# A gated delta-rule decoder layer: outputs and gate kept transposed, factors applied at the eviction, a new order on every queue

## The reference

```python
q, k, v = split(silu(conv4(x @ w_qkv)));  z = x @ w_z          # 16 q/k heads, 32 v heads, 128 channels each
for t in tokens:                                               # per batch and v head
    S = S * exp(g_t);  delta = (v_t - k_t S) * b_t
    S = S + outer(k_t, delta);  o_t = q_t S
og = o * silu(z)
on = og * rsqrt(mean(og * og, -1) + 1e-6) * norm_w
attention = on.reshape(B, T, 32 * 128) @ w_out                 # sum over heads
```

## Time and profile before

| | us |
|---|---|
| median of three runs (lowest, highest) | 2197.31 (2196.64, 2201.70) |
| the profiled execution, own time | 2197.97 |
| its span | 2196.2 |
| attention part, steady: first L1520 of m = 0 to that of m = 53 | 199.0 to 1428.9 |
| drain, to the first L1520 of m = 63 | 1428.9 to 1651.6 |
| cross attention and experts | 1651.6 to 2196.2 |

### The profile page before, as it was taken

One profiled execution on the slowest core, in us unless ns is written; L12 is line 12 of the kernel. 1 busy time (PEld: TensorE's weight loads), 2 busy tenths in 40 slices (PEclk: granted clock), 3 DMA queues, 4 the chain that ended last, 5 costly groups with the idle time before them and its releaser, 6 DMA issues.

```text
span 2196.2 us, 49295 instructions
## 1 busy us (share of the span) xinstructions
PE 2018.6 (92%) x18636; PEld 1681.6 (77%) x18636; DVE 1723.7 (78%) x2944; ACT 1497.9 (68%) x3523; POOL 893.3 (41%) x714
## 2 busy tenths in 40 slices
PE   4648999999999999999999999998878899999998
PEld 3437888888888888888888888887765567666676
DVE  6789798898988889898898988975236777767665
ACT  4536877778777787777878778765667666665632
POOL 1623454454454544544544545432343213322232
PEclk8869999999999999999999999998989999999999
DMA  3422323323233323323233232211342022222232
GB/s 79 96 70 50 81 57 69 83 55 67 63 74 71 68 65 67 74 65 75 64 61 79 63 70 71 42 49 48 87 148 87 1 97 73 82 96 97 83 129 87
DMA packets 274633, 161.56 MB, mean 74 GB/s; under 512 B 209352, under 2 KB 246752, under 8 KB 269280
## 3 DMA queue, kind: packets, MB, share of 16 engines
q1 hardware_dynamic: 274400, 158.41, 27.6%
HBM read 122.43 MB, written 35.91 MB: 72 GB/s over the span
## 4 chain that ended last, share of the span: by engine, by line
issue 35%; POOL 27%; PE 22%; DVE 9%; ACT 4%; DMA 2%; SPq 1%; POOLq 0%; DVEq 0%; ACTq 0%
POOL Q L557 5%; POOL SM L579 5%; POOL EB L495 5%; PE ps L1735 4%; POOL SZ L581 4%; PE ps L1351 3%; POOL EB L499 3%; PE ps L1352 2%; PE ps L1353 2%; POOL WL L473 2%; POOL SM L587 2%; ACT SC L860 2%; PE ps L1647 1%; PE ps L1656 1%; PE ps L1484 1%
## 5 line engine op out<-in xcount | busy, mean ns | idle before, releaser
L913 DVE SCALAR_TENSOR_TENSOR A<-ps,CW,A 128x508 f32<-128x508 f32 (+2 forms) x768 | 517.1, 735 | 62.7 <-ACT A L676 59.9
L574 POOL TENSOR_SCALAR SM<-SM 128x8 f32<-128x8 f32 x64 | 12.7, 198 | 746.8 <-ACT DL L695 746.8
L1351 PE MATMUL ps<-XH,WH 128*128 128x512 f32 x512 | 223.2, 436 | 31.9 <-DVE A L913 31.0
L1484 PE MATMUL ps<-WO,DL 128*128 128x256 f32 x1008 | 232.7, 384 | 19.0 <-ACT DL L682 11.6
L1484 PEld LDWEIGHTS ps<-WO,DL 128*128 128x128 f32 x1008 | 193.3, 193 | 47.9 <-ACT DL L682 13.4
L1353 PE MATMUL ps<-XH,WL 128*128 128x512 f32 x512 | 208.1, 407 | 0.0
L1352 PE MATMUL ps<-XL,WH 128*128 128x512 f32 x512 | 207.5, 405 | 0.0
L695 ACT ACTIVATE DL<-SZ 128x128 f32<-128x128 f32 x512 | 152.9, 300 | 59.4 <-issue 32.6
L1131 DVE TENSOR_TENSOR SZ<-SZ,ps 128x512 f32<-128x512 f32 x128 | 86.6, 687 | 128.4 <-PE ps L1520 126.9
L860 ACT ACTIVATE SC<-ps,A 128x128 f32<-128x128 f32 x512 | 142.2, 387 | 51.3 <-DVE A L1256 50.7
L1116 DVE TENSOR_TENSOR BP<-ps,EB 128x512 f32<-128x512 f32 x256 | 158.4, 682 | 2.6 <-ACT EB L667 2.6
(11 more groups left out here) (223 smaller groups left out, 5530.7 us busy)
## 6 DMA issues: line engine op xcount, KB each, us to landing
EB<-decay_rows SPq DMA_DIRECT2D x128, 256.0 KB, 4.6
WE<-expert_halves SPq DMA_DIRECT2D x32, 1024.0 KB, 5.1
x_blocks<-BP SPq DMA_DIRECT2D x256, 32.0 KB, 1.7
X<-x_blocks SPq DMA_DIRECT2D x16, 512.0 KB, 5.8
tt_blocks<-TI SPq DMA_DIRECT2D x16, 512.0 KB, 2.6
tn_blocks<-TM SPq DMA_DIRECT2D x16, 512.0 KB, 2.6
TTF<-tt_blocks SPq DMA_DIRECT2D x256, 32.0 KB, 1.9
expert_halves<-BP SPq DMA_DIRECT2D x8, 1024.0 KB, 5.5
```

What stands on the lines that cost most here:

```text
L913: dve.scalar_tensor_tensor(acc, ps(i, 0, [[128, 4], [1, 128 - s]]), at(CW, tile * 4 + 3 - s, [[1, 1]]), acc, ALU.mult, ALU.add).then_inc(s ...
L1351: pe.matmul(out, sa, ma, start=(kt == 0), stop=False)
L1484: t = pe.matmul(ps(7 - i, b * 256, [[1, 256]]), at(on_buf(k), (4 * i + 2 * b + v) * 128, [[1, 128]]), at(WO, v * 256, [[1, 256]]), start=( ...
```

## The change

z is computed transposed (weights stationary, 512 tokens moving; one bank for each head), the outputs too (deltas stationary), so that the gated output needs no transposing before the output projection. The factor 1/rms is not applied to it; PE projects each head by itself (no accumulation over the two heads; head 0 in banks 4 and 5, head 1 in 6 and 7), and the factor comes in at the eviction: ACT writes head 0 scaled to DL, POOL adds that to Y, DVE multiplies head 1 and adds it. The sums of squares over channels, which now lie on partitions, are made on PE with PICK, copied by ACT, transposed by PE, and scaled by DVE. The inverse's yields and the rooms of `pump` have other numbers, its copy to TM stands behind v's silu on ACT, the transposes for its norms ahead of the v projection, and on SP the loads are in another order. Cut to its core:

```diff
-        def on_buf(k):
-            return A2 if k == NSTEP - 2 else DL
+        def by_batch(t, off, i):
+            return at(t, off + i * 256, [[128, 2], [512, 2], [1, 128]])
+
+        def y_buf(k):
+            return DL if k < NSTEP - 2 else Q2
+
+        def o_bank(k, b, v):
+            return 6 + v if k >= NSTEP - 2 else 4 + 2 * v + b // 2
+
+        def o_count(k, b, v):
+            return 4 * k + (b // 2 * 2 + v if k >= NSTEP - 2 else 2 * v + b // 2) + 1
...
             load_wo(k // 4)
-        if n % 4 == 0 and 4 <= n <= NSTEP:
-            load_x(n // 4 - 1)
         if 0 <= m < NSTEP and m % 4 == 1 and m // 4 + 1 < HK:
...
             load_v(vn // 4 + 1)
-        if 0 <= wn < NSTEP and wn % 4 == 0:
-            store_t(wn // 4)
-        if 0 <= wn < NSTEP:
+        if 0 <= wn < NSTEP and wn % 4:
             load_ta(wn)
-            load_tt(wn)
+        if wn == 0:
+            store_t(0)
+            store_tn(0)
+            load_ta(0)
+            load_tt(0)
         if n < NSTEP:
...
             load_rows(n + 3)
+        if 0 < wn < NSTEP and wn % 4 == 0:
+            store_t(wn // 4)
+            store_tn(wn // 4)
+            load_ta(wn)
+        if n < NSTEP and n % 4 == 3:
+            load_x(n // 4)
+        if 0 < wn < NSTEP:
+            load_tt(wn)
         if n == NSTEP + 2:
...
+    def y_add(k):
+        yo = at(Y, 4 * (k % 4) * 256, full)
+        pool.wait_ge(sem["y_v0"], 4 * k + 4)
+        if k >= NSTEP - 2:
+            pool.wait_ge(sem["y_v1"], 4 * k + 4)
+        elif k >= 4:
+            pool.wait_ge(sem["y_v1"], 4 * (k - 4) + 4)
+        pool.tensor_tensor(yo, yo, at(y_buf(k), 0, full), ALU.add).then_inc(sem["y_add"], 1)
+
     def scale_wo(hk):
...
         s1, s3, sv = n < NSTEP, 0 <= m < NSTEP, 0 <= vn < NSTEP
+        if EARLY <= n and n + 2 < NSTEP:
+            decay(n + 2)
         if n % 4 == 3 and EARLY <= n and n + 1 < NSTEP:
             split_lo("kq", W_KQ, n // 4 + 1)
-        for e8 in SPLITS.get(n, ()):
-            split_raw_lo(e8)
-        if sv and vn % 4 == 3 and vn + 1 < NSTEP:
-            split_lo("v", W_V, vn // 4 + 1)
-        if s3 and m % 4 == 3 and m + 1 < NSTEP:
-            split_lo("z", W_Z, m // 4 + 1)
+        if 0 < k < NSTEP and k % 4 == 0:
+            scale_wo(k // 4)
+        if 0 <= k < NSTEP:
+            pool.wait_ge(sem["xs"], k + 1)
+            if k >= 2:
+                pool.wait_ge(sem["y_v0"], 4 * (k - 1))
+                pool.wait_ge(sem["y_v1"], 4 * (k - 1))
+            pool.tensor_tensor(at(SM, C_RR + 8 * (k % 2), [[1, 8]]), at(SM, C_XS, [[1, 8]]), at(SM, C_MH, [[1, 8]]),
+                               ALU.pow).then_inc(sem["rr"], 1)
         if n < EARLY:
...
                 split_lo("kq", W_KQ, n // 4 + 1)
...
         if s1:
...
             pool.tensor_tensor(at(Q2, 0, full), at(buf, 0, full), at(buf, 0, full), ALU.mult).then_inc(sem["sq"], 1)
-        if 0 < k < NSTEP and k % 4 == 0:
-            scale_wo(k // 4)
-        if EARLY - 1 <= n and n + 2 < NSTEP:
-            decay(n + 2)
...
+        if sv and vn % 4 == 3 and vn + 1 < NSTEP:
+            split_lo("v", W_V, vn // 4 + 1)
+        if s3 and m % 4 == 3 and m + 1 < NSTEP:
+            split_lo("z", W_Z, m // 4 + 1)
+        if 0 <= k < NSTEP - 2:
+            y_add(k)
+        for e8 in SPLITS.get(n, ()):
+            split_raw_lo(e8)
         if m == NSTEP - 1:
...
             block_keys(0)
-        if s3:
-            xs, rr, szp = at(SM, C_XS, [[1, 8]]), at(SM, C_RR, [[1, 8]]), at(SZ, (m % 2) * 1024, [[128, 8], [1, 128]])
-            xs2 = at(SM, C_XS, [[2, 4], [1, 2]])
-            pool.wait_ge(sem["ss"], 2 * m + 2)
-            pool.tensor_scalar(xs, at(SM, C_SS, [[1, 8]]), 1.0 / 128, 1.0, ALU.mult, ALU.mult).then_inc(sem["xs"], 1)
-            pool.wait_ge(sem["xs"], 2 * m + 1)
-            pool.wait_ge(sem["nq"], m // 4 + 1)
-            pool.tensor_tensor(xs2, xs2, at(SM, C_NQ + (m % RING) * 4, [[1, 4], [0, 2]]), ALU.add).then_inc(sem["xs"], 1)
-            pool.wait_ge(sem["xs"], 2 * m + 2)
-            pool.tensor_tensor(rr, xs, at(SM, C_MH, [[1, 8]]), ALU.pow).then_inc(sem["rr"], 1)
-            pool.wait_ge(sem["rr"], m + 1)
-            pool.tensor_tensor(szp, szp, at(SM, C_RR, [[1, 8], [0, 128]]), ALU.mult).then_inc(sem["on"], 1)
         if n % 4 == 0 and 4 <= n <= NSTEP:
...
-    def on_T(k, i):
-        act.wait_ge(sem["on_tr"], 2 * k + 1 + i)
-        act.wait_ge(sem["o_mm"], 2 * k + 2)
-        act.activation(at(on_buf(k), i * 512, [[1, 512]]), ps(4 + i), ACT.Copy).then_inc(sem["on_T"], 1)
+    def y_head(k):
+        act.wait_ge(sem["rr"], k + 1)
+        if k < NSTEP - 2:
+            act.wait_ge(sem["og_mm"], k + 1)
+        else:
+            act.wait_ge(sem["nq_mm"], NSTEP)
+        if k:
+            act.wait_ge(sem["y_add"], k)
+        for b in range(4):
+            act.wait_ge(sem["out_mm"], o_count(k, b, 0))
+            act.activation(at(y_buf(k), b * 256, [[1, 256]]), ps(o_bank(k, b, 0), b % 2 * 256, [[1, 256]]), ACT.Copy,
+                           scale=at(SM, C_RR + 8 * (k % 2) + 2 * b, [[1, 1]])).then_inc(sem["y_v0"], 1)
...
         act.wait_ge(sem["og"], 2 * m + 1 + i)
...
-        for pr in range(4 * i, 4 * i + 4):
-            t = act.activation(at(DL, pr * 128, [[1, 128]]), at(SZ, (m % 2) * 1024 + pr * 128, [[1, 128]]),
-                               ACT.Square, accum_out=at(SM, C_SS + pr, [[1, 1]]))
-        t.then_inc(sem["ss"], 1)
+        act.wait_ge(sem["o_mm"], 2 * m + 1 + i)
+        act.activation(at(DL, i * 512, [[256, 2], [128, 2], [1, 128]]), by_batch(SZ, (m % 2) * 1024, i),
+                       ACT.Square).then_inc(sem["og_sq"], 1)
...
         s1, s3, s4, sv = n < NSTEP, 0 <= m < NSTEP, 0 <= k < NSTEP, 0 <= vn < NSTEP
+        if s3 and m:
+            squares(m - 1, 1)
         if n % 4 == 3 and EARLY <= n and n + 1 < NSTEP:
             split_hi("kq", W_KQ, n // 4 + 1)
+        if s4:
+            act.wait_ge(sem["og_mm"], k + 1)
+            if k:
+                act.wait_ge(sem["og_tr"], k)
+            act.activation(at(RRW, 0, [[1, 128]]), ps(2, 0, [[1, 128]]), ACT.Copy).then_inc(sem["og_row"], 1)
         if sv:
...
                                scale=-1.0).then_inc(sem["u1_sb"], 1)
-        if s3 and m:
-            squares(m - 1, 1)
         if s1:
...
                            ACT.Copy).then_inc(sem["tt128_sb"], 1)
+        if s4 and k < NSTEP - 2:
+            y_head(k)
         if not s1 and sv and vn % 4 == 3 and vn + 1 < NSTEP:
...
             decay_exp(n + 1)
-        if s4 and k < NSTEP - 1:
-            on_T(k, 0)
-        if 0 <= wn < NSTEP and wn % 4 == 0:
-            act.wait_ge(sem["inv"], INV_OPS * (wn // 4 + 1))
-            act.activation(at(TM, 0, [[1, 32], [32, 32]]), at(TI, 0, [[32, 32], [1, 32]]), ACT.Copy).then_inc(sem["tn"], 1)
-        if s4 and k < NSTEP - 1:
-            on_T(k, 1)
         if EARLY <= n and n % 2 == 0 and n + 1 < NSTEP:
...
             act.activation(at(A2, 0, full), at(A2, 0, full), ACT.Silu).then_inc(sem["v_silu"], 1)
+        if 0 <= wn < NSTEP and wn % 4 == 0:
+            act.wait_ge(sem["inv"], INV_OPS * (wn // 4 + 1))
+            act.activation(at(TM, 0, [[1, 32], [32, 32]]), at(TI, 0, [[32, 32], [1, 32]]), ACT.Copy).then_inc(sem["tn"], 1)
         if s3:
             if s4:
-                act.wait_ge(sem["out_mm"], 2 * k + 2 if m < NSTEP - 1 else 2 * k)
+                act.wait_ge(sem["og_mm"], k + 1)
+            if 0 <= k < NSTEP - 2:
+                act.wait_ge(sem["y_add"], k + 1)
             for i in range(2):
...
+    def mult_ns(n):
+        return 150 + 1.05 * n
+
+    def sum_ns(n):
+        return 180 + 1.72 * n
+
     def inverse(j):
...
-    def y_add(k, i):
-        yo = at(Y, (4 * (k % 4) + 2 * i) * 256, [[1, 512]])
-        dve.wait_ge(sem["out_mm"], 2 * k + 1 + i)
-        if k >= 4:
-            dve.wait_ge(sem["y_add"], 2 * (k - 4) + 1 + i)
-        dve.tensor_tensor(yo, yo, ps(7 - i), ALU.add).then_inc(sem["y_add"], 1)
+    def y_head(k):
+        dve.wait_ge(sem["rr"], k + 1)
+        if k < NSTEP - 2:
+            dve.wait_ge(sem["y_add"], k + 1)
+        else:
+            dve.wait_ge(sem["y_v1"], 4 * (k - 4) + 4)
+        for b in range(4):
+            yo = y_row(4 * (k % 4) + b)
+            dve.wait_ge(sem["out_mm"], o_count(k, b, 1))
+            dve.scalar_tensor_tensor(yo, ps(o_bank(k, b, 1), b % 2 * 256, [[1, 256]]), at(SM, C_RR + 8 * (k % 2) + 2 * b + 1, [[1, 1]]),
+                                     yo, ALU.mult, ALU.add).then_inc(sem["y_v1"], 1)
     def gate(m, i):
-        dve.wait_ge(sem["z_silu"], 2 * m + 1 + i)
+        z = at(SZ, (m % 2) * 1024 + i * 256, [[512, 2], [1, 256]])
+        dve.wait_ge(sem["z_silu"], 2 * m + 2)
         dve.wait_ge(sem["o_mm"], 2 * m + 1 + i)
-        dve.tensor_tensor(z_half(m, i), z_half(m, i), ps(6 + i), ALU.mult).then_inc(sem["og"], 1)
+        dve.tensor_tensor(z, z, ps(6 + i, 0, [[256, 2], [1, 256]]), ALU.mult).then_inc(sem["og"], 1)
+
+    def mean_squares(k):
```

(133 more changed lines are left out.)

78 lines of the change are left out of this document (38 added, 40 removed).

## The result

The changed kernel takes **2300.2 us** in the median of four runs (2297.2 to 2303.3); the kernel before, 2198.5. The ratio is 1.046, with a 95% interval from 1.044 to 1.048: 102 us slower, where 20 us faster was forecast. The profiled execution took 2303.27 us, with a span of 2301.4.

| stretch | before | after | difference | forecast |
|---|---|---|---|---|
| ramp, to the outputs of step 0 | 199.0 | 202.1 | +3.1 | 0 |
| steady, outputs of step 0 to 52 | 1206.5 | 1303.1 | +96.6 | +1 |
| drain, outputs of step 52 to 63 | 246.1 | 239.3 | -6.8 | -22 (of the part from 53: measured -6.0) |
| tail | 544.6 | 556.8 | +12.2 | +1 |

What follows compares the result with a forecast made beforehand. The steady part was taken as PE-bound with a small unevenness, the drain as bound by waits in a chain over all engines. Steady +1, drain -22, tail +1 gave -20 us from 2197.97: 2177 us, range 2134 to 2210.

Steps and rivals of the forecast that it cites:

- the TM copy: Once in four steps: store lands at 23.3 us, reload ends at 26, wanted at 26.5; in time, barely.
- the load of X: Block load for the next inverse, behind the reload on SP: lands about when DVE wants it; 0, at worst 1 us.
- level with PE, with no reserve: DVE, steady part: load 21.1 us a step, 95% of 22.27; averaged over four steps it doesn't bind.
- PE's work: Steady part, per step: -0.45 us, between -0.2 and -0.6; 22.72 becomes 22.27.
- Even steps: ACT's evictions ahead of exponentials and v's silu: +1.0 us in each even step, +2.0 per four, between 0 and 3.6.
- the -1.65: Steady part, per four steps: PE's waits for POOL's scaling (L1467) and DVE's gate (L1539) go, -1.65 us.
- The copy behind v's silu: ACT, once in four steps: outputs wait 0.9 us, z 0.7; +1.6, between 0 and 3.1.
- Drain: End of the attention part: waits for L682, w_out and L581 go; -22 us, between -30 and -5; sign: under 205 us.
- Scaled w_out's 6.6: Drain: PE's 6.6 us wait for w_out's scaling, queued on POOL behind weight splitting, goes as scaling comes first.
- Tail: First scores wait for bank 2, about +2.5 us; up to 2 comes back from last outputs without transposes: +1.
- B: Rival, every step: ACT's chain becomes the bound, 2215 us; sign: mean step over 23.5 us; chance 0.16.
- C: Rival: POOL and DVE block each other beside parts of the inverse, 0.3 us a step, +16, 2194 us; chance 0.07.

Runs made afterwards that it cites:

- e3: Changed kernel with the TM copy right behind the tt128 eviction and SP's order of the kernel before: 2266.9 us.
- e5: Changed kernel with the TM copy behind the tt128 eviction, inverse stores and TA load ahead of x stores, X load right behind them, TTF load last: 2256.6 us.
- e12: e3 with the inverse started behind v's first taps and its rooms refitted, exponentials behind y_head as in the change: 2221.7 us.
- e2: Changed kernel with only SP's order of the kernel before; TM copy stays behind v's silu: 2377.0 us.
- e6: e3 with the inverse started behind v's first taps, metering left as in the changed kernel: 2353.3 us.
- e8: Changed kernel with the earlier SP order, inverse metering, rooms and start, and the TM copy behind the tt128 eviction: 2238.6 us.
- e9: e5 with the inverse's first piece behind v's third taps and that step's TTF load right behind the TA load: 2278.5 us.
- e1: Changed kernel with only the TM copy moved, to right behind the tt128 eviction: 2312.7 us.
- e10: e9 with exponentials ahead of y_head in even steps and, in the drain, more inverse ahead of mean_squares, less ahead of the gates: 2264.8 us.
- e13: e11 with POOL making the squares of q and k twice per step: 2279.9 us.
- e15: e12 with POOL making the squares of q and k behind y_add, not ahead of it: 2232.1 us.
- e11: e3 with the inverse started behind v's first taps, its rooms refitted, and exponentials ahead of y_head in even steps: 2252.8 us.

## Why the prediction was wrong

**The step that failed** is this one of the TM copy: "Its store then lands at 23.3 (2.6); a reload that takes as long at most ends at 26, and the next step's first small matmuls want it at 26.5: in time, barely". The copy itself ended where I had it, 20.7 us in (748.1, where 26.5 is 753.9). But the 2.6 us was measured with an empty queue, and I used it for a store that the same diff puts behind x stores, two row loads and the store of TI. It took 5.5 in this round, 5.2 to 8.1 in 13 of 16. "As long at most" for the reload had no row behind it, and was wrong too: it took 3.5 here, and mostly 3.5 to 4.0 in the trace of before. The margin was 0.5 us, so a term that I put at 0 was a wait of 3.3 us, and what comes with it, the clock above all, was 3.4 more. I had the diff's new order of SP in front of me and priced only what was behind, not what was beside.

What this step is worth in the total: with TA in time (e3) 33 us come back, with X in time as well (e5) 44, of the 123 between forecast and result. In the steady part alone, the profiled executions give 47 of 97 back in e5, and another 18 in e12, whose inverse starts behind v's first taps with rooms of its own; 32 stay.

**The second half of that sentence**, the load of X "0, at worst 1 us", held in the changed kernel, where that load stands ahead of the step that wants it. e2 and e3 show its price when it is late.

**The start of the inverse ahead of v's taps** had no term at all. I divided the inverse evenly over DVE's steps and found DVE "level with PE, with no reserve"; "averaged over four steps it doesn't bind" is the sentence that fell. DVE is in order, so in that one step it waits for norms, a transpose and X with v's taps behind it. e6 moves this start behind the first taps, and the long step falls from 29.8 us to 23.6, with a new one elsewhere; e8 and e12, with the same start, have it at 23.6 too. e9, which only moves the first piece behind the third taps, leaves it at 27.1 for 27.3.

**Terms that held.** PE's work: 22.27 was forecast for an undisturbed odd step, 22.3 to 22.4 measured. Even steps +1.0: 23.5 in most versions with the exponentials behind y_head (n mod 4 = 2), so +1.2; 22.8 with them ahead. L1467's wait did go; L1539's for the gate went, but the squares of the gated output brought one as long (3.7 us for 3.5 from 600 to 1200 us), which the -1.65 doesn't have. The copy behind v's silu in its own step: 1.6 forecast, 0.9 measured (23.3 against 22.4 in e1).

**Drain.** -22 forecast, -6.0 measured for the same part. L682's and L581's waits went. Scaled w_out's 6.6 didn't: PE waited 7.4 us for it again, since POOL now waits for the load of w_out itself, and the projection follows at once. The trace of before could have told: there the load landed at 1601.9 and the scaling began at 1602.4, so the splitting ahead of it on POOL held it up by 0.5 us of the 6.6. And a new wait came, for the gates' squares: DVE has up to 5.8 us of inverse ahead of the gates (a room of 2900, doubled in the drain). With less there, the drain is 228 to 231 in e10 to e13 and e15, -15 to -18. (Waits of PE in the drain, 1527 to 1745 us, as the earlier trace rows.)

```profile
PE ps L1680 <- ACT DL L870: 14.6, 9, 3.3
PE ps L1462 <- ACT DL L733: 13.7, 4, 5.8
PE ps L1544 <- POOL WO L517: 7.4, 1, 7.4
```

**Tail.** +1 forecast, +12.2 measured, and 10 to 15 in every run with the new output path. The last two steps' projections share banks 6 and 7, so each half waits for the eviction of the one before it (1744 to 1800 us):

```profile
PE ps L1544 <- ACT Q L721: 9.3, 2, 6.8
```

I read the edit to these banks and looked only at bank 2. This is read from the trace, not tested by a run.

**Rivals.** The result is slower than B's 2215, and the mean step of 25.1 us is past the 23.5 that I had named as B's sign, but B's mechanism isn't behind it: ACT's chain costs even steps 1.2 us for the forecast 1.0. The drain's sign, under 205 us, failed as well: 216.7. C, POOL and DVE blocking each other, was priced at 0.3 us a step; by the sums above the changed kernel has 30 us more of it than the one before. How much of that is on the path no run shows: e15 moved it and got slower, and e13 adds other delays with it. The rule that I cited for it (the Trainium skill, SBUF — State Buffer, Who interferes with whom) agrees with e13's products. The other rule of the Trainium skill that I cited (ScalarE: Activation LUTs, What ACT_TABLE_LOAD costs), a drain of about 1380 ns at a table load, doesn't show in the changed kernel either: the silu at 723.66 starts 0.01 us behind its load of 1.28 us, and even steps are 1.2 us longer than odd ones, where by that rule they would be 2.8 longer still.

**What stays open.** The steady part of e12 takes 95.3 us per four steps, where two of 22.4 and two of 23.5 would make 91.8. The difference of 3.5 lies in the step behind the start of an inverse, 25.8 us for 22.4. What its trace shows there from 600 to 1200 us, each once in a round: PE waits 9.5 us in six times for v's taps on DVE, and 4.3 in six for the squares of the gated output, since DVE has work of the inverse ahead of the taps and of the gates. Products beside POOL lengthen that work. No run separates its amount from its slowing.

## What to carry to other kernels

A landing time belongs to the queue in which it was measured: when a diff reorders a queue, price each transfer with its new neighbours, and treat a margin smaller than that difference as a miss. On an engine that works in order, an average load says nothing about a piece with its own late inputs (here the start of the inverse): write down what it waits for and what stands behind it. When edits belong together, such as an earlier start and an earlier load, undoing one makes things worse and doesn't refute the theory; undo them as a set.

## What the runs showed of the hardware

- The same 512 KB store lands in 2.6 us (before, e2, e3), in 5.4 (median of the changed kernel; up to 8.1) or in 7.0 (median of e1; up to 8.2). e2 changes only SP's order and brings it back to 2.6. In the changed kernel an equal store was issued 1.5 us and two row loads up to 2.5 us ahead of it, in e1 the equal store 0.5 us ahead.
- A gap of 3.3 us in PE's work was followed by some 8 us at a granted clock of 0.61 in the mean; 512-column matmuls start 0.43 us apart there (763.44, 763.87) for 0.23. There 2.7 us were lost to the clock for 3.3 to the gap itself. The same came in 13 rounds: gaps of 2.2 to 5.2 us, each with 3.4 to 10.2 us at the lower level behind it.
- DVE's two-operand instructions on SBUF can be held up for about as long as a POOL instruction takes: 128x16 elements at 1.73 us for 0.19 in e13. So can a copy with one operand in SBUF: 0.62 for 0.18. The taps and other instructions with an operand in PSUM keep their time to within 1%, and the sums to within 4% (e11 and e13).
